# Transposes of x ahead of the scores, the context split one half later, scales spread by transposes

## What is computed

```python
def xattn(x, ctx):                       # x is layernormed
    q_in = x @ Wq + lora(x)              # 256 -> 1024
    k_in, v_in = org_ctx @ Wk + lora, org_ctx @ Wv + lora
    out = attention(q_in, k_in, v_in) + attention(q_in, ipa_ctx @ Wk_ipa, ipa_ctx @ Wv_ipa)
    return out @ Wo + bo + lora(out)
def ffn(x):                              # x is layernormed
    h = bit_linear(x, w1)                # activations rounded to 8 bits per token, weights ternary
    h = silu(depthwise_conv1d(h, conv_w, conv_b))
    return bit_linear(h, w2)
x = x + xattn(layernorm(x), ctx)
x = x + ffn(layernorm(x))
```

## Time and profile before

| | |
|---|---|
| median of 3 runs | 1571.66 us (1570.8 to 1572.26) |
| the profiled execution | 1570.99 us, of which the trace's span is 1569.0 us |
| busy: PE / DVE / ACT / POOL | 1441.2 / 1214.9 / 1177.5 / 660.0 us |
| PE weight loads | 1174.6 us |
| mean granted TensorE clock | 0.975 |
| moved by DMA | 47.13 MB, mean 30 GB/s |

### The profile page before, as it was taken

The page is one execution under the profiler, slowest core; times in us unless marked ns, Lnnn a source line. Parts: engine busy times, 40 slices in busy tenths (PEclk is TensorE's granted clock), DMA queues, the critical chain, the costliest instruction groups (busy, mean ns, idle before and its releaser), DMA issues.

```text
span 1569.0 us, 33374 instructions
## 1 busy us (share of the span) xinstructions
PE 1441.2 (92%) x10778; PEld 1174.6 (75%) x10778; DVE 1214.9 (77%) x3059; ACT 1177.5 (75%) x3909; POOL 660.0 (42%) x1058
## 2 busy tenths in 40 slices
PE   7899999999999999999999999999999999998743
PEld 4688788787878878787877878787887878787621
DVE  4364797887879798787969888786978878786966
ACT  3487887968778796978878797887879787787721
POOL 2354444434444443445344444444444344444500
PEclk9999999999999999999999999999999999999965
DMA  9100001000000100000010100000010100000000
GB/s 280 44 30 27 19 15 45 15 29 14 28 29 14 43 14 31 13 28 29 18 38 14 43 0 28 29 28 29 14 43 9 34 14 28 29 1 28 1 14 13
DMA packets 41128, 47.13 MB, mean 30 GB/s; under 512 B 3008, under 2 KB 35200, under 8 KB 41088
## 3 DMA queue, kind: packets, MB, share of 16 engines
q1 hardware_dynamic: 41088, 46.62, 9.8%
HBM read 36.13 MB, written 10.49 MB: 30 GB/s over the span
## 4 chain that ended last, share of the span: by engine, by line
PE 52%; ACT 20%; DVE 19%; issue 9%; DMA 0%; DVEq 0%; ACTq 0%; POOL 0%; SPq 0%; POOLq 0%
PE PS L478 10%; ACT SM L675 8%; PE PS L440 8%; PE PS L491 6%; PE PS L421 5%; PE PS L456 5%; PE PS L465 4%; PE PS L430 4%; PE PS L539 4%; ACT HP L696 2%; DVE GBS L887 2%; PE PS L518 2%; DVE GBS L908 2%; ACT GBS L701 2%; ACT QM L642 2%
## 5 line engine op out<-in xcount | busy, mean ns | idle before, releaser
L1053 POOL TENSOR_TENSOR SM<-SM,RC 128x496 f32<-128x496 f32 (+1 forms) x512 | 331.6, 668 | 747.8 <-DVE RC L822 742.1
L675 ACT ACTIVATE SM<-PS,MX 128x124 f32<-128x124 f32 x1024 | 358.7, 366 | 147.9 <-DVE SM L828 145.8
L478 PE MATMUL PS<-KT,QM 128*128 128x128 f32 x2048 | 278.2, 279 | 29.3 <-ACT SM L675 29.2
L478 PEld LDWEIGHTS PS<-KT,QM 128*128 128x128 f32 x2048 | 249.4, 192 | 44.8 <-ACT SM L675 44.5
L675 ACT ACTIVATION_READ_ACCUMULATOR SM<-PS,MX 128x1 f32 x1024 | 212.9, 208 | 0.0
L1084 POOL TENSOR_TENSOR OTl<-OF,OTh 128x256 fp32r<-128x256 f32 x256 | 196.0, 766 | 14.6 <-ACT OF L669 14.6
L667 ACT ACTIVATE OTh<-PS 128x256 fp32r<-128x256 f32 x256 | 100.4, 392 | 116.3 <-PE PS L456 115.1
L465 PE MATMUL PS<-IDF,SM 128*128 128x128 f32 x1024 | 168.4, 287 | 8.1 <-POOL SM L1053 8.0
L826 DVE TENSOR_REDUCE MX<-PS 128x4 f32<-128x496 f32 x256 | 170.1, 664 | 0.2 <-issue 0.2
L456 PE MATMUL PS<-PT,V 128*64 128x128 f32 x2048 | 168.8, 286 | 0.1
L456 PEld LDWEIGHTS PS<-PT,V 128*64 128x64 f32 x2048 | 106.8, 136 | 81.9 <-issue 74.9
(11 more groups left out here) (142 smaller groups left out, 3566.4 us busy)
## 6 DMA issues: line engine op xcount, KB each, us to landing
XIN<-in_x SPq DMA_DIRECT2D x16, 512.0 KB, 3.6
XRES<-in_x SPq DMA_DIRECT2D x16, 512.0 KB, 3.6
out_y<-HP SPq DMA_DIRECT2D x16, 512.0 KB, 3.0
CRAW<-in_ctxT SPq DMA_DIRECT2D x16, 256.0 KB, 2.7
RRAW<-in_ctxT SPq DMA_DIRECT2D x32, 128.0 KB, 2.9
QM<-in_Wq SPq DMA_DIRECT2D x1, 1024.0 KB, 9.4
GBS<-in_Wo SPq DMA_DIRECT2D x1, 1024.0 KB, 14.1
k_ipa_columns<-HP SPq DMA_DIRECT2D x1, 1024.0 KB, 6.6
```

The lines of the kernel that those rows point to most:

```text
L478: m = mm(psS[:, h, :], QM[:, 2 * q + h // 2, h % 2, TOK * b:TOK * b + TOK], KT[:, 2 * q + h // 2, b, :], start=True, stop=True)
L675: m = act.activation(SM[s % 2][:, h, 0:ORG], psS[:, h, 0:ORG], ACT.Exp, bias=MX[s % 2][:, h:h + 1], accum_out=SU[s % 2][:, h:h + 1])
L1053: m = pool.tensor_tensor(part, part, RC[c % 2][:, 4 * i:4 * i + 4].unsqueeze(2).broadcast_to(shape), ALU.mult)
```

## The change

Edits of order, and one of operation:

- PE: the transposes of x leave `project` and stand between `transpose_p` and `scores` of half 8.
- ACT: the copy of the second V tile of a quad stands ahead of the output copies of its half (this matters in halves 0 and 8). The high parts of the context move from half 8 to half 9, behind the exponentials.
- DVE: the split of the context moves from half 8 to half 10 (N_CSPLIT[1]), behind `attend` of that half. M_SCALE moves the scales from half 10 to half 11; nothing of DVE stands between, so in its order they stand right behind the split.
- The work before the loop follows the same numbers: for the first group, XTh and XTl now stand ahead of the context's parts on ACT and DVE.
- SP: the transfer of the K columns, which waits for `c_split`, moves from half 10 to 11. POOL: their copies into KT move from halves 13, 21, 28, 36 to 15, 23, 30, 38.
- PE: both spreads of scales become transposes (4 instructions each where there were 8).

```diff
--- before.py
+++ after.py
@@ -55,14 +55,15 @@
 N_STATS, N_VAR, N_POW, N_NORM = 0, 3, 4, 6
 N_XT = 8
 N_CIN = 7
-N_CSPLIT = 8
-N_KI = 10
+N_CSPLIT = (9, 10)
+N_KI = 11
+N_KIPA = 15
 N_Q, N_K, N_V = (10, 14), (11, 15), (13, 16)
 N_QUAD = (0, 8, 15, 23)
 TERNARY = 5
 TERNARY_SUM = TERNARY + 4
 M_FIN = 2
-M_SCALE = 1
+M_SCALE = 2
 EARLY_HALVES = N_XT + 2
 
 M_X2 = (4, 7)
@@ -401,7 +402,7 @@
                 need(pe, unit_free[u % 2], g.count(UNITS // 2, u // 2))
                 return psU[u % 2]
 
-            def project(g, n):
+            def transpose_x(g, n):
                 if n == N_XT:
                     pe.wait_ge(ln1_done, g.count(1, 1))
                     for k in range(2):
@@ -409,6 +410,8 @@
                         for b in range(NB):
                             m = pe.transpose(bank[:, TOK * b:TOK * b + TOK], XIN[:, b, P * k:P * k + P], IDF[:])
                         m.then_inc(unit_full, 1)
+
+            def project(g, n):
                 for a in range(2):
                     q = quad_at(n - N_Q[a])
                     if q is not None:
@@ -506,7 +509,7 @@
                     pe.wait_ge(scale_done, g.count(2, 1))
                     pe.wait_ge(q1t_done, g.count(1, 1))
                     for b in range(NB):
-                        m = mm(psF[:, TOK * b:TOK * b + TOK], AD[0][:, b:b + 1].broadcast_to([P, P]), IDF[:], start=True, stop=True)
+                        m = pe.transpose(psF[:, TOK * b:TOK * b + TOK], AD[0][:, b:b + 1].broadcast_to([P, P]), IDF[:])
                     m.then_inc(bc_full, 1)
                 j = tile_at(n - M_F1)
                 if 0 <= j < CT:
@@ -525,7 +528,7 @@
                 if n == M_BC2:
                     pe.wait_ge(scale_done, g.count(2, 2))
                     for b in range(NB):
-                        m = mm(psF[:, TOK * b:TOK * b + TOK], AS[1][:, b:b + 1].broadcast_to([P, P]), IDF[:], start=True, stop=True)
+                        m = pe.transpose(psF[:, TOK * b:TOK * b + TOK], AS[1][:, b:b + 1].broadcast_to([P, P]), IDF[:])
                     m.then_inc(bc_full, 1)
                 for c in range(2):
                     if n == M_F2[c]:
@@ -575,6 +578,7 @@
             for i in range(PAIRS):
                 ipa_product(i)
             for n in range(EARLY_HALVES):
+                transpose_x(At(0), n)
                 project(At(0), n)
             pe.wait_ge(w_in[5], 2 * 16)
             for i in range(PAIRS, 12):
@@ -606,6 +610,8 @@
                 if n % 2 == 0:
                     p_v(g, n // 2)
                     transpose_p(g, n // 2)
+                    if g.shift(1).exists(1):
+                        transpose_x(g.shift(1), n)
                     scores(g, n // 2)
                     project_out(g, n // 2)
                 if g.reg is None:
@@ -625,7 +631,7 @@
         @block.scalar
         def _(act):
             def project(g, n):
-                if n == N_CSPLIT:
+                if n == N_CSPLIT[0]:
                     act.wait_ge(c_in, g.count(48, 48))
                     need(act, unit_full, g.count(UNITS, 0))
                     act.activation(CTH[0][:], CRAW[:], ACT.Identity)
@@ -647,6 +653,8 @@
                         act.wait_ge(unit_full, g.count(UNITS, u + 1))
                         act.activation(KT[:, 2 * q + a, :, 0:ORG], psU[u % 2].rearrange("p (b t) -> p b t", b=NB)[:, :, 0:ORG],
                                        ACT.Identity).then_inc(unit_free[u % 2], 1)
+
+            def value_copy(g, n):
                 q = quad_at(n - N_V[1] - 1)
                 if q is not None:
                     u = 2 + 6 * q + U_V[1]
@@ -729,6 +737,7 @@
             act.wait_ge(w_low, 4)
             act.wait_ge(wv_low, 2)
             for n in range(EARLY_HALVES, HALVES):
+                value_copy(At(0), n)
                 project(At(0), n)
                 if n == LORA_O + 1:
                     high_part(6)
@@ -736,6 +745,10 @@
             act.wait_ge(small_in[2], 5 * 16)
 
             def steps(g, n):
+                if g.exists():
+                    value_copy(g, n + HALVES)
+                if g.shift(1).exists(1):
+                    value_copy(g.shift(1), n)
                 if n % 2 == 0:
                     output_copies(g, n // 2)
                     transposed_copy(g, n // 2)
@@ -798,7 +811,7 @@
                 if n == N_NORM:
                     dve.wait_ge(ln1_rstd, g.count(1, 1))
                     normalise(0, XIN, XIN).then_inc(ln1_done, 1)
-                if n == N_CSPLIT:
+                if n == N_CSPLIT[1]:
                     dve.wait_ge(c_high, g.count(1, 1))
                     dve.tensor_tensor(CTH[1][:], CRAW[:], CTH[0][:].bitcast(F32), ALU.subtract)
                     dve.tensor_tensor(CTR[64:128, :], RRAW[64:128, :], CTR[64:128, :].bitcast(F32), ALU.subtract).then_inc(c_split, 1)
@@ -912,7 +925,7 @@
                         dve.tensor_scalar(Q2[j], GB[j % 4].rearrange("p b t -> p (b t)"), MAGIC, MAGIC,
                                           ALU.add, ALU.subtract).then_inc(q2_done, 1)
 
-            for n in range(EARLY_HALVES):
+            for n in range(EARLY_HALVES + 1):
                 project(At(0), n)
 
 
@@ -948,7 +961,7 @@
                     low_part(1)
             low_part(2)
             low_part(4)
-            for n in range(EARLY_HALVES, HALVES):
+            for n in range(EARLY_HALVES + 1, HALVES):
                 project(At(0), n)
                 if n == LORA_O + 1:
                     dve.wait_ge(w_in[2], 16)
@@ -1034,7 +1047,7 @@
                 if n == N_POW:
                     pool.wait_ge(ln1_var, g.count(1, 1))
                     pool.tensor_tensor(RS[0][:], VE[0][:], HALF[:], ALU.pow).then_inc(ln1_rstd, 1)
-                q = quad_at(n - N_V[0])
+                q = quad_at(n - N_KIPA)
                 if q is not None:
                     pool.wait_ge(ki_in, g.count(16, 16))
                     need(pool, s_full, g.count(CHUNKS, 4 * q + NB - CHUNKS))
```

## The result

| | before | after |
|---|---|---|
| median (us) | 1571.23 (1570.67 to 1572.26, 4 runs) | 1599.14 (1593.66 to 1601.65, 4 runs) |
| ratio | 1 | 1.0172, 95% interval 1.0142 to 1.0203 |
| the profiled execution | 1570.99, span 1569.0 | 1593.66, span 1591.7 |

The change costs 28 us. Its lines stand 3 further on for PE (433 is 430, 481 is 478), and mostly 13 further on for DVE and POOL.

What follows compares the result with a forecast made beforehand. PE was taken to bound the kernel, with DVE gapless from half 8's maxima to the scales. Terms: 21.4 + 0.4 - 1.9 = 19.9, plus clock 16.8, +36.7 us on 1570.99: about 1608, stated 1607, range 1586 to 1616 us.

Steps and rivals of the forecast that it cites:

- Transposes and maxima: PE, half 8: transposes of x take 0.97 us ahead of the scores, so DVE's maxima start at 708.24 instead of 707.27.
- Exponentials: ACT: freed from four copies but waiting for later maxima; gain 0.3 us taken, PE's wait of 0.95 becoming 0.65.
- The split: DVE, half 10: ends at 716.21, first K tile at 716.25, PE idle about 2.5 us, round 1.66 us late.
- The rest of the round: PE after half 12's scores: no wait to give before the first spread; DVE's and ACT's later work shifts with PE.
- I take 0: SP's K-column transfer and context transfer and POOL's K copies, all later: no cost, since their readers have time to spare.
- Spreads: PE, scales by transposes: first gains nothing in a round, second 0.13 us; last group 2 x 0.93 = 1.9 us.
- Round without the clock: One round where the clock stays at full rate: 91.9 us, against 90.35 before the change.
- the sum's 1.53: Added time per round at full clock, 1.66 - 0.13 = 1.53 us, in rounds 1 to 14: 21.4 us.
- The clock: PE's new idle time lets its clock fall in some rounds: 1.2 us per round on average, 14 x 1.2 = 16.8 us.
- A: Rival: the K tile waits but PE's clock holds, 1571.7 + 19.9 = 1592 us; chance 0.24.
- B: Rival: the K tile waits and the clock falls at nearly every wait, 14 x 2.7 = 37.8 us, 1629 us; chance 0.08.
- Absorption (C): Rival: PE catches up the 1.66 us in its later waits of 2.2 us, leaving the spreads' gain, 1557 us; chance 0.10.

Runs made afterwards that it cites:

- the filled wait: The changed kernel with 24 small unused bf16 products on PE ahead of the first K tile in rounds 1 to 14: 1582.47 us, ratio 1.0072.

## Why the prediction came out as it did

Forecast 1607 in 1586 to 1616, measured 1599: the mechanism and sign held, one term that was put at nothing wasn't nothing, and one that came out right was partly luck.

- **Transposes and maxima.** 0.97 us was said; the scores start 0.87 us behind the transposes (810.05 to 810.92), and the maxima come at 812.02 - 103.87 = 708.15, against 708.24. Shown alone: +0.62 a round.
- **Exponentials.** Gain of 0.3 said, 0.37 measured; the wait of 0.95 became 0.57 where 0.65 was said.
- **The split.** K tile 716.25 said, 716.22 measured; wait of about 2.5 said, 2.39 measured; split alone +1.00, and +0.98 with the rest. The round's lag at half 12 was to be 1.66. It is 1.63, by the scores further on (826.94 in the changed kernel against 721.44 before), and 0.62 + 1.00 from the single parts.
- **The rest of the round.** "From there to the first spread PE has no wait to give" held, and the lag of 1.63 lasts to half 22. "I take 0" for POOL's move was the step that failed: the K copies give 0.38 us, by a wait of PE for DVE's V copy that stands behind slowed products. I had read POOL's queue for its readers only, not for what runs beside it.
- **Spreads.** First 0, as said. Second 0.13 said, about 0.2 measured (0.17 alone, 0.22 in the changed kernel, 0.19 with the additions). End: 2 x 0.93 said, 0.96 and 0.97 measured.
- **Round without the clock.** 91.9 said, 91.37 measured: 1.63 - 0.40 - 0.22 = 1.01 against 1.02. Against the sum's 1.53 that is 0.51 less, over 14 rounds 7.1 us, most of the 8 us by which the forecast was high. Another 1.7 us came at the very end, where the last products ran at full clock; the forecast had no such term. The profiled execution comes out of these parts: 14 x 1.02 + 8 x 1.50 - 1.9 - 1.7 = 22.7 us, which is what its span grew by.
- **The clock.** 1.2 us a round said, as a mean over rounds that fall and rounds that don't. Profiled: 8 falls of 1.50 in 14 rounds, 0.86 a round. If the other executions differ only in the number of falls, the median's 5.5 us above the profiled one are some 4 more, 1.2 to 1.3 a round. That was not seen in a trace, but their mean granted clocks go with it: 0.970, 0.968, 0.963 and 0.963 at 1593.66, 1596.89, 1601.38 and 1601.65 us. The two slowest are 8 us above the profiled one, by this estimate 5 more falls, so that the clock fell at about every one of the 13 full waits. Their spread is 8 us, where before's is 1.6. That the wait sets it off is shown by the filled wait. That 1.2 was so near was luck in part: it was picked between 0 and 2.7, with neither the price of a fall nor their number worked out. The rows it was picked from held less than it read in them: 2.5 us is not as long as the longest waits of that trace, which has one of 10.00 in the earlier trace rows; and a fall in the loop is shorter than what the earlier trace rows show: the clock is at 0.50 of its full rate from 727.4 to 730.8 only, which the expectation of a sooner recovery had right. Of the rivals, A's "clock holds" is the filled kernel's 1582: A at 1592 was too dear by the POOL term and the end. B's condition, a fall at nearly every wait, may have held in the two slowest executions, but its price of 2.7 never showed; a fall costs 1.50.
- **Absorption (C).** What came back in the round is 0.62 us, but not by the mechanism of C: PE's waits in the feed-forward part stayed. It came from edits of the same change that help by themselves.

Singly the parts make +0.62, +0.62 (split with K copies) and -0.17, sum +1.07 against +1.02 measured: they simply add. One change held two losing and two gaining edits.

## What to carry to other kernels

Where an engine that is not the busiest has no gap between two points at which the busiest waits for it, count its work between them: putting a job later there makes one consumer wait, and moving another out of the way can make the next one wait (here 2.39 us became 0.71 and 2.05). Test a change of many edits by its parts before it is dropped: its K copies, spreads and V copy alone were 0.8% faster than before, and the spreads with an edit that the experiments suggested, the moved additions, 1%. When POOL's instructions move, look at which two-input products of DVE they then lie on, not only at who reads them.

## What was not expected of the hardware

- **DVE and POOL slow each other.** A product of DVE with two inputs takes 0.68 us at 740.19 and 1.20 at 743.35 beside POOL's subtraction and addition; the addition takes 1.17 there and has a mean of 0.73 in its other place. The Trainium skill, "SBUF — State Buffer", section "SBUF: two separate sides", has DVE and GpSimd share a pair of ports as an exclusive lock: a DVE operation with two SBUF inputs and a GpSimd operation that reads SBUF exclude each other, and whichever starts first keeps the ports to its end. The traces agree as far as they go: DVE's product of line 887, one of whose inputs is in PSUM, has a mean of 0.683 us over all 128, before as after, where the two lines with both inputs in SBUF have 0.866 and 0.929. Which of the two engines is held each time was not tried.
- **The clock falls after a wait of 2.4 us in the midst of a full engine, and not every time.** Same wait, same work, and mostly every second round falls; ahead of the K tile at 1.38 and 1.03 us it did in none. In the kernel with the late layernorm it falls in 3 of 14 rounds at waits of 2.05 us. The length of the wait alone doesn't decide: near the end of the changed kernel, where PE was busy for 3.48 of 5.50 us (1466.0 to 1471.5), the clock fell right behind a wait of 1.44 us. 1.36 us of idle products in the wait keep it up and save 17 us.
- **The end runs at either clock.** In the last group the changed kernel's last products ran at 2.4 GHz (1.92 us for 16) where before they took 3.60, which gave 1.7 us. They took 1.92 us in seven of the nine kernels that spread the scales by transposes, and over 3.5 in the other two and in all five that do not; what decides it was not tested. PE's timeline, after and before:

```profile
1585.44 1.92 PE L542 MATMUL PS<-W,HP 128*128 128x256 bf16 x16 [0.97 <-DVE HP L851]
```

```profile
1561.12 3.60 PE L539 MATMUL PS<-W,HP 128*128 128x256 bf16 x16 [0.97 <-DVE HP L838]
```
